# Two sets of accumulator banks, the last layer's work reordered, and eight pairs written out

## The reference

```python
scores = leaky(si[:, :, None] + sj[:, None, :] + attn_b[l])      # slope 0.2
attn = softmax(where(mask, scores, -inf), axis=-1)
h = layernorm(x + attn @ x, g1[l], beta1[l])
x = layernorm(h + gelu(h @ W1[l] + b1[l]) @ W2[l] + b2[l], g2[l], beta2[l])
# second network, on h = relu(layernorm(x_in + x)):
Wh = h @ W
e = where(adj > 0, leaky(Wh @ a1 [:, None] + Wh @ a2 [None, :]), -9e15)
out = x + leaky(softmax(e, axis=1) @ Wh)
```

## Time and profile before

| | us |
|---|---|
| median of 3 runs | 2248.99 (2244.24 to 2250.16) |
| the profiled execution | 2248.39 |
| its span, first to last instruction | 2246.6 |
| PE busy in it | 1910.3 |
| DVE busy in it | 1726.7 |
| mean granted clock of TensorE | 0.964 |

### The profile page before, as it was taken

How to read it: one execution, slowest core, us unless ns; L and a number is a source line. 1 busy time by engine, 2 the same in 40 slices (tenths; PEclk the granted TensorE clock), 3 DMA queues, 4 the chain that set the end, 5 groups by cost and what they waited for, 6 DMA issues and landing times.

```text
span 2246.6 us, 33876 instructions
## 1 busy us (share of the span) xinstructions
PE 1910.3 (85%) x11009; PEld 1622.3 (72%) x11009; DVE 1726.7 (77%) x5021; ACT 1169.1 (52%) x1844; POOL 929.3 (41%) x657
## 2 busy tenths in 40 slices
PE   3888888988888889889889898898888988898884
PEld 2777767777777767778777776777767777777773
DVE  6677887688877887778877787877887779877754
ACT  2554555555555555555555554655545555555542
POOL 2355443334433444344434343443443434433442
PEclk9899999999999999999999999999999999999997
DMA  4001100011000110001000010000100010000000
GB/s 150 20 29 39 37 10 20 1 38 39 2 19 1 43 34 2 20 1 57 20 2 19 12 56 11 1 20 20 48 12 11 10 38 29 10 10 1 29 1 19
DMA packets 40526, 52.82 MB, mean 24 GB/s; under 512 B 2911, under 2 KB 30857, under 8 KB 40329
## 3 DMA queue, kind: packets, MB, share of 16 engines
q1 hardware_dynamic: 40328, 50.37, 7.0%
HBM read 41.97 MB, written 8.39 MB: 22 GB/s over the span
## 4 chain that ended last, share of the span: by engine, by line
PE 40%; DVE 22%; issue 16%; POOL 14%; ACT 7%; DMA 1%; POOLq 0%; ACTq 0%; SPq 0%; DVEq 0%
PE ps_d L475 10%; PE ps_a L412 9%; PE ps_a L505 5%; PE ps_u L451 5%; DVE probs L993 3%; POOL probs L1195 3%; DVE junk L925 3%; PE ps_a L491 3%; POOL gelu_lo L1189 2%; POOL columns L1156 2%; PE ps_t L421 2%; ACT normed L642 2%; POOL x_nat L1165 2%; ACT g_full L661 2%; DVE probs L989 2%
## 5 line engine op out<-in xcount | busy, mean ns | idle before, releaser
L475 PE MATMUL ps_d<-w_hi,gelu_hi 128*128 128x256 f32 x1536 | 473.2, 308 | 37.3 <-POOL gelu_lo L1189 26.2
L661 ACT ACTIVATE g_full<-ps_u,vec_all 128x512 f32<-128x512 f32 x384 | 259.4, 688 | 365.7 <-PE ps_u L451 156.1
L475 PE MATMUL ps_d<-w_hi,gelu_lo 128*128 128x256 f32 x1536 | 435.6, 284 | 0.0
L475 PE MATMUL ps_d<-w_lo,gelu_hi 128*128 128x256 f32 x1536 | 435.2, 283 | 0.0
L412 PE MATMUL ps_a<-x_nat,probs 128*128 128x257 f32 x1536 | 381.0, 401 | 54.2 <-ACT probs L636 37.5
L1189 POOL TENSOR_TENSOR gelu_lo<-g_full,gelu_hi 128x512 fp32r<-128x512 f32 x240 | 315.2, 1319 | 231.9 <-ACT gelu_hi L669 172.6
L412 PEld LDWEIGHTS ps_a<-x_nat,probs 128*128 128x128 f32 x1536 | 293.4, 198 | 136.6 <-ACT probs L636 64.1
L1156 POOL TENSOR_TENSOR columns<-columns 128x4 f32<-128x4 f32 x128 | 133.8, 1045 | 616.2 <-DVE columns L784 616.2
L475 PEld LDWEIGHTS ps_d<-w_hi,gelu_hi 128*128 128x128 f32 x1536 | 294.8, 192 | 53.7 <-POOL gelu_lo L1189 34.1
L475 PEld LDWEIGHTS ps_d<-w_lo,gelu_hi 128*128 128x128 f32 x1536 | 295.3, 192 | 5.8
L475 PEld LDWEIGHTS ps_d<-w_hi,gelu_lo 128*128 128x128 f32 x1536 | 293.4, 191 | 0.0
(11 more groups left out here) (123 smaller groups left out, 3743.8 us busy)
## 6 DMA issues: line engine op xcount, KB each, us to landing
adj_in<-adj_dram SPq DMA_DIRECT2D x64, 256.0 KB, 2.7
x_nat<-x_dram SPq DMA_DIRECT2D x16, 512.0 KB, 3.7
x_res<-x_dram SPq DMA_DIRECT2D x16, 512.0 KB, 3.7
out_dram<-x_res SPq DMA_DIRECT2D x64, 128.0 KB, 1.7
x_res<-L_gnn_W_dram SPq DMA_DIRECT2D x5, 1024.0 KB, 5.1
probs<-L_gnn_W_dram SPq DMA_DIRECT2D x1, 1024.0 KB, 9.8
attn_row<-L_gnn_attn_w_dram SPq DMA_DIRECT2D x1, 768.0 KB
g_row<-L_gnn_g_dram SPq DMA_DIRECT2D x1, 384.0 KB
```

Source lines behind the costliest of these rows:

```text
L475: last = pe.matmul(ps_d[c // 2][:, cols:cols + D], h[:, r, tok], w[:, layer, f, :], start=False, stop=(f == FC - 1 and i == 2), skip_group ...
L661: full = act.activation(g_full[:, f % 2, :], ps_u[f % 2][:, :], ACT.Gelu, bias=b1_col[:, layer, f:f + 1])
```

## The change

`ps_d` and `ps_a` become `acc[side][0..1]`: each side has two banks, which hold its attention sums, then its `down` sums; the second network uses the banks of the side that is not in `down`. The second network's order changes: `final_norm` has columns of its own (`mean_g`, `rstd_g`); `final_turn` and `project` stand before `attend_out`, `final_rows` after it; `final_bounded` is done whole at the end of slots 0 and 2, with `h_rest` inside it; `final_exps` stands after `h_split` there; `final_scale` is in `ff_norm` of the late slot; `final_out` follows `up` 4, with `scores_row` in its midst. ACT takes the factor 0.2 of `final_leaky` (`output_low`) and the copy in `final_mask` (`keep_mask`). ACT does both halves of `ff_apply` after gelu 2. `mask_transposes` uses the free side's banks, before the last `down`, with the copies after `h_split`. On DVE, mask chunks stand later in slots 4 and 5 and gelu remainder 4 after `bounded_scores` where `layer_a` is 0; on POOL, gelu remainder 2 stands before `layer_input`, `residual_shift` right after it. All eight pairs are straight code on every engine. Below, `...` stands also for removed lines of functions that the listing above shows.

```diff
 ps_u = [bank("ps_u0"), bank("ps_u1")]
-ps_d = [bank("ps_d0"), bank("ps_d1")]
-ps_a = [bank("ps_a0"), bank("ps_a1")]
+acc = [[bank("acc00"), bank("acc01")], [bank("acc10"), bank("acc11")]]
 ps_t = [bank("ps_t0"), bank("ps_t1")]
...
-def each_pair(engine, body):
-    body(0, True, PAIRS == 1)
-    if PAIRS > 2:
-        with engine.Fori(1, PAIRS - 1) as pair:
-            body(pair, False, False)
-    if PAIRS > 1:
-        body(PAIRS - 1, False, True)
+def each_pair(body):
+    for pair in range(PAIRS):
+        body(pair, pair == 0, pair == PAIRS - 1)
 class Slot:
...
+    def attend_out(n, side, layer, g):
+        if begun(ln2_apply.at(n - 2)):
+            pe.wait_ge(ln2_apply.sem, ln2_apply.at(n - 2))
         if layer == 0:
             pe.wait_ge(x0_ready.sem, x0_ready.at(g))
...
-        dst = ps_d[c // 2]
+        dst = acc[side][c // 2]
         for k in range(KC):
             pe.matmul(dst[:, cols + k * P:cols + (k + 1) * P], h_full[:, k, c * P:(c + 1) * P], ident[:, :],
                       start=(c % 2 == 0 and k == 0), stop=False, is_transpose=True, skip_group_check=True)
...
-                residual(n, layer, c)
+                if rows_of is not None and c == 2:
+                    pe.wait_ge(g_q.sem, g_q.at(rows_of))
+                if masks_of is not None and c % 2 == 0:
+                    pe.wait_ge(mask_ready.sem, mask_ready.at(masks_of, c + 2))
+                residual(n, side, c)
             cols = (c % 2) * D
             tok = slice(c * P, (c + 1) * P)
             for i, (h, w) in enumerate(((gelu_hi, w2_hi), (gelu_hi, w2_lo), (gelu_lo, w2_hi))):
-                last = pe.matmul(ps_d[c // 2][:, cols:cols + D], h[:, r, tok], w[:, layer, f, :],
...
+    def final_turn(g, banks, n):
+        pe.wait_ge(ln2_apply.sem, ln2_apply.at(n - 1))
+        turn_tokens(wh, lng_apply, g_tr, g, banks)
...
+    def slot(s, pair):
+        n, side, layer, other = s.n, s.side, s.layer, s.other
+        free = acc[other]
+        soon = s.layer_a == 0 and not s.begins
+        graph_a = s.first_x if s.begins else s.ff_graph + 2 if s.ff_graph is not None else None
+        start_of(s, pair)
+        if s.late is not None:
+            pe.wait_ge(ln2_apply.sem, ln2_apply.at(n - 1))
+            final_out(s.late[0], free, (0, 1))
+        if not soon:
             scores_row(n + 1)
...
         if s.late is not None:
...
+            final_out(s.late[0], free, (2, 3))
+        early_turn = s.final is not None and not soon
+        if early_turn:
+            final_turn(s.final[0], free, n)
+        if soon:
+            bound_rows(n + 1)
+        down(n, side, layer, 2)
+        if early_turn:
+            project(s.final[0], free)
         up(n, layer, 5)
...
+        if not soon:
+            bound_rows(n + 1)
+        if s.final is not None and soon:
+            final_turn(s.final[0], free, n)
+        down(n, side, layer, 3)
+        if s.final is not None and soon:
+            project(s.final[0], free)
         up(n, layer, 6)
...
+        if s.prepare is not None and side == 0:
+            down(n, side, layer, 4)
+        if s.late is not None:
+            pe.wait_ge(o_leaky.sem, o_leaky.at(s.late[0]))
+        attend_out(n + 1, other, s.layer_a, graph_a)
+        if not (s.prepare is not None and side == 0):
+            down(n, side, layer, 4)
+        if s.final is not None:
+            pe.wait_ge(y_ready.sem, y_ready.at(n + 1))
+            final_rows(s.final[0], free)
+        up(n, layer, 7)
+        down(n, side, layer, 5)
         pe.wait_ge(q_ready.sem, q_ready.at(n + 1))
...
+        turn_tokens(normed, ln1_apply, h_tr, n + 1, ps_t)
+        down(n, side, layer, 6)
         if s.prepare is not None:
...
+            mask_transposes(s.prepare, side, free)
+        down(n, side, layer, 7)
+    def closing_slot(s, pair):
+        n, side, layer = s.n, s.side, s.layer
+        free = acc[s.other]
+        start_of(s, pair)
+        down(n, side, layer, 2)
+        up(n, layer, 5)
+        down(n, side, layer, 3)
+        up(n, layer, 6)
+        down(n, side, layer, 4)
+        final_turn(s.ff_graph, free, n)
         up(n, layer, 7)
...
...
+    def keep_mask(g, side):
+        act.activation(mask_g[:, side, :, :], mask_t[:, side, :, :], ACT.Copy).then_inc(mask_copied.sem, 1)
...
+    def output_low(g, banks):
+        for c in range(NC):
+            act.wait_ge(o_done.sem, o_done.at(g, c + 1))
+            if c >= 2:
+                act.wait_ge(o_ready.sem, o_ready.at(g, c - 1))
+            elif begun(o_ready.at(g - 1)):
+                act.wait_ge(o_ready.sem, o_ready.at(g - 1))
+            act.activation(o_tmp[:, c % 2, :], banks[c % 2][:, 0:D], ACT.Copy, scale=SLOPE).then_inc(o_low.sem, 1)
...
             gelu(n, layer, 2)
             if not s.begins:
...
+                ff_apply(n - 1, other, 0)
+                ff_apply(n - 1, other, 1)
+            if s.keep is not None:
+                keep_mask(*s.keep)
             if s.begins:
                 input_apply(s.first_x, 1)
             gelu(n, layer, 3)
...
                 gelu(n, layer, 7)
+                final_wh(s.ff_graph, free)
+                final_low(s.ff_graph, free)
+                final_exps(s.ff_graph)
                 continue
+            if s.late is not None:
+                output_low(s.late[0], free)
+            if s.final is not None and s.layer_a > 0:
+                final_h(s.final[0], free)
+                final_wh(s.final[0], free)
             low_row(n + 1)
+            if s.final is not None and s.layer_a == 0:
+                final_h(s.final[0], free)
+                final_wh(s.final[0], free)
             exps(n + 1)
             gelu(n, layer, 5)
             if s.prepare is not None:
                 input_apply(s.prepare, s.side)
             gelu(n, layer, 6)
             if s.final is not None:
...
+                final_low(s.final[0], free)
+            gelu(n, layer, 7)
+            h_split(n + 1, s.layer_a)
+            if s.final is not None:
+                final_exps(s.final[0])
             if s.prepare is not None:
...
+                mask_copies(s.prepare, s.side, free)
+    each_pair(pair_body)
+    ff_apply(B * LAYERS - 1, 1, 0)
+    ff_apply(B * LAYERS - 1, 1, 1)
+    output_low(B - 2, acc[0])
+    final_h(B - 1, acc[0])
...
             gelu_high(n + 1)
...
+        if late is not None:
+            final_scale(late)
         def half(b):
             chunks = (2 * b, 2 * b + 1)
...
                                      op0=ALU.mult, op1=ALU.mult).then_inc(ln2_shift.sem, 1)
         half(0)
+        if follows and scores is not None:
+            gelu_rest(n + 1, 1)
         half(1)
+        if follows and scores is None:
+            gelu_rest(n + 1, 1)
         if scores is not None:
             step_next, layer, turn = scores
             for t in (1, 0):
...
+    def final_bounded(g, side, banks, step=None):
...
         dve.tensor_scalar(sg_j8[:, :], wh[:, :, D + 1], 1.0 - SLOPE, None, ALU.mult).then_inc(sg_scaled.sem, 1)
         dve.wait_ge(sg_scaled.sem, sg_scaled.at(g))
...
+        scores(0)
+        for j in range(NC - 1):
+            dve.wait_ge(g_q.sem, g_q.at(g, j + 1))
+            scores(j + 1)
+            greatest(j)
+            if j > 0:
+                negate(j - 1)
+        if step is not None:
+            h_rest(*step)
+        dve.wait_ge(g_q.sem, g_q.at(g))
+        negate(NC - 2)
+        greatest(NC - 1)
+        negate(NC - 1)
...
                 input_shift(s.first_x)
                 layer_scores(n + 1, 1, s.first_x)
             else:
...
+                ff_norm(n - 1, other, (n + 1, s.layer_a, s.turn) if s.attend and s.layer_a > 0 else None, True,
+                        s.late[0] if s.late is not None else None)
             if not s.attend:
                 gelu_rest(n, 3)
                 gelu_rest(n, 4)
                 final_norm(s.ff_graph, 0, n - 1)
...
+                final_apply(s.ff_graph, 0)
+                final_bounded(s.ff_graph, 0, free)
                 continue
...
+            if s.late is not None:
+                final_leaky(s.late[0], free, (0, 1))
+            if s.final is not None and s.layer_a > 0:
+                final_apply(*s.final)
+            neighbour_max(n + 1, other)
+            if s.late is not None:
+                final_leaky(s.late[0], free, (2, 3))
             if s.keep is not None:
                 final_mask(*s.keep)
...
+            if s.final is not None and s.layer_a == 0:
+                final_norm(*s.stats)
+                gelu_rest(n, 3)
+                final_apply(*s.final)
+            else:
+                if s.prepare is not None and s.side == 1:
+                    prepare_masks(s.prepare, 1, (0,))
+                gelu_rest(n, 3)
+            if s.layer_a > 0 or s.begins:
+                gelu_rest(n, 4)
+            bounded_scores(n + 1, other, s.late[0] if s.late is not None else None)
+            if s.layer_a == 0 and not s.begins:
+                gelu_rest(n, 4)
```

(18 more changed lines are left out.)

350 lines of the change are left out of this document (116 added, 234 removed).

## The result

The changed kernel takes 2214.8 us, median of 4 runs (2211.49 to 2218.18), the kernel before 2246.89 beside it. The ratio is 0.9861, 95% interval 0.9847 to 0.9875: 1.4% or 31 us faster. Forecast were 113 us. The direction is right and the time lies in the range (2080 to 2230), but the forecast gain is more than three times the measured one.

The account below looks back on a forecast made before the run. PE was taken as the bound, busy 1910.3 of 2246.6 us, so only its 336 us of pauses could go. Gains of 11.5 (loop), 72 (six middle pairs), 15 (pair 0) and 15 (pair 7) made 113.5: 2135 us, range 2080 to 2230.

Parts of the forecast that it names:

- (b): Slots 0 and 2: nearly all of final_bounded now precedes h_rest, costing 0.7 us a slot, 1.4 a middle pair.
- (f): final_h and final_wh before the exponentials delay them about as much as project delays attend_out: cost 0.
- The loop: Writing out the loop over the middle pairs removes five turns of 2.3 us each: 11.5 us gained.
- Residual waits: h_full transposes no longer wait for ff_apply, which read the same banks: 1.45 us a slot, 8.7 a middle pair gained.
- Late scale: In late slots final_out no longer waits for final_scale: 2.75 us each, 5.5 a middle pair gained.
- slot 5: Attention's wait for the first exponentials, behind four mask chunks on DVE, goes: 4.0 us gained; slot near 41.5 us.
- Step (a): Exponentials at the end of slots 0 and 2 delay the next slot's gelu 0: 3.2 us each, 6.4 a middle pair.
- Step (c): Slot 5: two mask chunks between bounding and attention_sum cost 2.4 us, the last chunk another 1.0: 3.4.
- The tail: After pair 7's last slot: 5.8 us before final_out and the last turn's wait go, final_norm costs 3.5; net 7 gained.
- Rival 2: At slot edges POOL holds up DVE's bounding reductions: 9.6 us in each of 14 late slots, 2269 us; chance 0.11.
- Rival 4: Straight code runs out of instructions, losing the loop's gain and more: about 2250 us; chance 0.04, shared with a cancelling of all.
- Rival 3: Only the loop and the tail pay, the order moving waits without removing them: 2230 us; chance 0.18.

Follow-up runs that it names:

- e4: The changed kernel with GpSimd starting layer_input in slots 0 and 2 only after VectorE's final_apply of the same slot: 2167.7 us, 0.962 of the kernel before.
- e13: The changed kernel with GpSimd's layer_input waiting for final_apply in slot 0 alone: 2173.57 us, 0.9657 of the kernel before.
- e5: e4 with scores_row put back between down 0 and down 1 in slots 2 and 4 and in pair 0: 2160.43 us, 0.9599.
- e11: e9 with GpSimd's layer_input in slots 4 and 5 begun only after neighbour_max's row chain, and residual_shift after mask_scores: 2144.54 us, 0.9547.
- e1: The kernel before with only its loop over the six middle pairs written out on every engine: 2232.34 us, 0.9914.
- e3: The changed kernel with TensorE's h_full transposes again waiting for ff_apply of the step before: 2266.86 us, 1.0068 of the kernel before.
- e14: The changed kernel with final_exps after gelu 1 of the late slot and final_scale at the end of ff_norm: 2176.24 us, 0.967.
- e10: e9 with mask chunk 2 of slots 4 and 5 moved to between attention_sum and attention_norm: 2104.5 us, 0.9368.
- e6: e4 with the transposes of mask chunks 0 to 2 ahead of the turn of the tokens in slots 4 and 5: 2160.35 us, 0.9599.
- e15: e10 with GpSimd's last gelu remainder of a slot begun only after attention_norm: 2098.16 us, 0.932.
- e8: e4 with final_exps after gelu 1 of the late slot and final_scale at the end of ff_norm: 2129.89 us, 0.9464.
- e9: The changed kernel with the edits of e4, e5, e6 and e8 together: 2124.63 us, 0.9453 of the kernel before.
- e2: The changed kernel with the loop over the six middle pairs put back: 2237.79 us, 0.9943 of the kernel before.

## Why the prediction was wrong

A slot is taken here from its first matmul to that of the next slot. The table has the mean over pairs 1 to 6 of both traces, and what the prediction's own terms add up to for that slot (with the loop in slot 5).

| slot | before, us | after, us | measured change | forecast change |
|---|---|---|---|---|
| 0 | 42.3 | 45.4 | +3.1 | -0.8 |
| 1 | 48.1 | 47.7 | -0.4 | -1.0 |
| 2 | 43.3 | 42.2 | -1.0 | -2.1 |
| 3 | 48.2 | 46.5 | -1.7 | -1.0 |
| 4 | 40.7 | 42.0 | +1.3 | -3.3 |
| 5 | 47.4 | 42.1 | -5.3 | -5.7 |

So slots 0 and 4 carry most of what is missing.

- **The step that failed** is one that has no letter: "`final_turn` and `project` stand before `attend_out`" was priced only by what follows it, (b) and (f). `final_apply` had to move with them, from `attention_sum` up to a place between `ff_norm` and bounding, where GpSimd is in `layer_input`. There it takes 5.53 us, where it takes 1.38 alone (e4) and took 2.4 at its old place, on the chain of everything in the slot: 54 us by e4, 46 of them by the wait in slot 0 alone (e13). The prediction named the rule of the Trainium skill (SBUF — State Buffer, "SBUF: two separate sides") for two inputs in SBUF, and asked it only of the bounding's reductions. The same section puts VectorE's two-port modes under that lock as well, and the Trainium skill (VectorE: DVE Perf Modes, "What auto-detection actually checks") gives such a mode to an instruction whose single source and destination lie in SBUF, as those of `final_apply` do. The trace agrees, 5.53 us beside GpSimd and 1.38 without.
- **Two more moves without a term**, in slots 4 and 5. `scores_row` went behind `up` 4 in slot 4, and `bound_rows` ahead of `down` 2 in slot 5. PE now waits there for VectorE's row chain in `neighbour_max`. The waits for it in the whole run, before and after, and the two in pair 3 after:

```profile
PE ps_t L370 <- DVE columns L834: 9.3, 11, 5.3
...
PE ps_t L378 <- DVE columns L879: 47.0, 20, 5.4
```
```profile
1043.13 1.10 PE L378 MATMUL ps_t<-ident,columns 128*128 128x128 f32 x8 [2.50 <-DVE columns L879]
...
1081.29 1.69 PE L378 MATMUL ps_t<-ident,columns 128*128 128x128 f32 x8 [2.82 <-DVE columns L879]
```

In slot 5 the chain starts 9.4 us into the slot, 9.6 before, so there it is the earlier place of `bound_rows` that makes it wait. What these waits cost is not shown: e5 put `scores_row` back and gained 5 us, and e11 freed the chain and lost by it elsewhere.
- **The loop**, 11.5 us: 19 (e1). Five turns were counted and six pairs pay, and 2.3 us was read from pair 6 alone, whose slot 5 (45.3 us) is itself 0.6 longer than e1's mean.
- **Residual waits**, 67 us over the pairs: 47 at most by e3, which makes the wait longer than it was. The wait is gone from the trace, and its own length over-states it.
- **Late scale**, **slot 5**: as forecast. No wait of `final_out` for `final_scale` in a late slot is left, and slot 5 is at 41.6 to 43.1 us (41.5 forecast, before the 47.6 of the earlier trace rows).
- **Step (a)**, 3.2 us a late slot: 2.96 measured, with gelu 0 of slot 1 at +5.8 us, where +6 was forecast. It was named the least trusted step, and it held. Taking it away gave 43 us in 14 slots, 3.1 each, the clock and what came back elsewhere included (e14).
- **Step (c)**, 2.4 us before PE's third chunk in slot 5: 1.94. Right; but moving one chunk (e10) gave 19 us, most of it in slot 4.
- **Step (f)**, 0: right as it stands, since with `final_apply` free (e4) PE has no pause over 0.5 us in slot 0 of pair 3, and the slot is 40.3 us, shorter than the 42.4 of the earlier trace rows.
- **No term for the clock.** PE was busy 22.3 us longer with the same matmuls. The forecast even leaned the other way (a higher clock from fewer pauses). Slot 4 had a granted clock of 1.00 in every pair before, and has 0.96 in all but the last; slot 1 fell from 0.96 to 0.93 in six of seven pairs; slot 0 has 0.96 in all seven, where three had 1.00.
- **The tail**, 7 us: 3.2 (91.9 to 88.7). The turn that was to wait no longer still waits 2.3 us for `final_apply` (1.53 and 0.77). PE pauses 7.23 us before the first `final_out`, where 5.2 were to be left. The 3.5 us for the moved statistics came as charged (the pause before the last turn went from 1.30 to 4.70). And PE is busy 2.4 us longer.
- Rival 2, the edge as the bound, is the nearest in kind (VectorE operations held by GpSimd), in another place. Rival 4 is excluded by e1. Rival 3's 2230 us is the nearest in size. Its reason holds in part: the waits before `bound_rows` are waits that moved, but e3 shows that the order did remove others.

The experiments' gains can't be summed up to the 82 us that were missing. With e4's 54 us slots 0 and 2 become shorter than forecast (40.3 and 40.7 us, forecast 41.5 and 41.1), so other terms there were worth more than they were priced at. What can be said is this: `final_apply` beside `layer_input` cost 54 us, more than any other single thing; the residual waits were priced at least 20 us too high and the loop 8 too low; and slot 4, 4.6 us a pair above its forecast, shows new pauses in its trace (2.50 before `bound_rows`, and 2.25 before the turn of the tokens, where it was 1.60), but which of the moves made it so long stays open. e5, e6 and e10 show only that its length is tied to slot 5's.

The best version, e15, which holds the edits of e4, e5, e6, e8 and e10 as well, runs in 2098 us, 6.8% faster than before.

## What to carry to other kernels

When an edit moves an operation on VectorE, look up what GpSimd does at its new place, for every operation that is moved and not only for the ones that the edit is about; a long GpSimd operation is best put where the VectorE operation beside it has time. Look the same way at every row that moved on TensorE: when it comes later, so does the chain that reads it, and when it comes earlier, what it reads may not be ready. Price a pause of TensorE by its length and by the clock of the few microseconds behind it. Before several edits are summed, check that the same slot isn't held by another engine's list: gains in one slot may only move the time into the next. And compare the mean of all pairs: one pair may be the mild case.

## What the runs showed of the hardware that I had not expected

- A pause of 2.96 us, at a clock that fell to 0.91 on average, was followed by 2.6 us at 0.50 (1.2 GHz). For the same 11009 matmuls PE was busy 1947.6 us in e3 (clock 0.950), 1932.6 in the changed kernel (0.953), 1914.4 in e4 (0.960), 1885.2 in e10 (0.982). The sum of the pauses alone doesn't tell it: the kernel before paused for 336 us and was busy 1910.3 (0.964), the changed kernel paused for 284 and was busy 1932.6.
- A VectorE operation of 128x4 elements that takes 0.16 us took 2.38 beside GpSimd's `layer_input` (e9), and one of 128x512 that takes 0.69 took 2.84 beside `residual_shift` (e11). Both lost about 2.2 us, close to the length of GpSimd's operation (2.40 and 2.80), whatever the size of VectorE's.
- A turn of the loop over all engines cost 3.1 us in slot 5, and the entry into it 2.9, in the old order (e1); in the new order 2.5 and nothing that shows in slot 5 (e2).
